# Two 64-row matmuls in place of two 128-row matmuls for the expert shift of the first phase

## What is computed

```python
logits = (jnp.einsum('tzd,ed->tze', x, phi_w) + phi_b).reshape(t, z, n, p)   # n = 64 experts, p = 32 slots
D = jax.nn.softmax(logits, axis=3)       # over the slots of an expert
C = jax.nn.softmax(logits, axis=2)       # over the experts of a slot
X_tilde = jnp.einsum('tznp,tzd->npd', D, x)
```

## Time and profile before

| | |
|---|---|
| median of 3 runs | 1187.13 us |
| span of the profiled execution, first to last instruction | 1184.2 us |
| runs above that span | 2.9 us |
| TensorE busy | 1144.7 us, 97% |
| VectorE busy | 1050.1 us, 89% |
| ScalarE busy | 981.7 us, 83% |
| GpSimd busy | 958.9 us, 81% |

### The profile page before, as it was taken

How to read it: one execution, slowest core, us unless ns; L and a number is a source line. 1 busy time by engine, 2 the same in 40 slices (tenths; PEclk the granted TensorE clock), 3 DMA queues, 4 the chain that set the end, 5 groups by cost and what they waited for, 6 DMA issues and landing times. The chain is left out here.

```text
span 1184.2 us, 17639 instructions
## 1 busy us (share of the span) xinstructions
PE 1144.7 (97%) x5097; PEld 787.9 (67%) x5097; DVE 1050.1 (89%) x1608; ACT 981.7 (83%) x2128; POOL 958.9 (81%) x770
## 2 busy tenths in 40 slices
PE   5999999999999999999989999999999999999996
PEld 3666666565666666666457777777777777777764
DVE  7999999999999999999767888888888888888887
ACT  5877877877766766766668999999999999999998
POOL 3998999898999999999788777878777788877751
PEclk9999999999999999999999999999999999999999
DMA  4445435434424432443754444344444444444420
GB/s 131 152 152 200 141 140 182 153 128 164 155 109 160 155 133 113 161 156 129 225 188 154 131 142 143 119 147 128 142 143 143 131 128 134 141 128 142 142 72 18
DMA packets 125263, 167.36 MB, mean 141 GB/s; under 512 B 7536, under 2 KB 102000, under 8 KB 125040
## 3 DMA queue, kind: packets, MB, share of 16 engines
q1 hardware_dynamic: 123984, 165.71, 41.4%
q10 hardware_dynamic: 1184, 0.53, 0.2%
HBM read 90.71 MB, written 75.50 MB: 140 GB/s over the span
## 5 line engine op out<-in xcount | busy, mean ns | idle before, releaser
L146 POOL TENSOR_TENSOR exp_slots_loaded<-exp_slots_loaded,slot_max 128x1024 f32<-128x1024 f32 x128 | 323.2, 2545 | 6.6 <-DMA exp_slots_loaded<-exp_slots 3.2
L858 POOL TENSOR_TENSOR dd<-ed,rz 128x512 f32<-128x512 f32 x256 | 267.6, 1051 | 24.7 <-ACT rz L688 23.4
L563 PE MATMUL acc<-dd,xns 128*128 128x512 f32 x512 | 261.1, 592 | 0.7 <-POOL dd L858 0.7
L1917 DVE TENSOR_TENSOR clo<-ct,chi 128x512 fp32r<-128x512 f32 x256 | 171.5, 681 | 24.3 <-ACT chi L1585 21.6
L176 POOL TENSOR_TENSOR ch<-exp_slots_loaded 128x512 f32<-128x512 f32 x128 | 165.9, 1296 | 32.0 <-ACT exp_slots_loaded L666 30.9
L795 DVE TENSOR_REDUCE mr<-lg 128x16 fp32r<-128x512 f32 x256 | 168.0, 685 | 19.3 <-PE lg L506 16.9
L657 ACT ACTIVATE ed<-lg 128x512 f32<-128x512 f32 x256 | 145.6, 594 | 40.3 <-PE lg L540 38.4
L666 ACT ACTIVATE exp_slots_loaded<-lg 128x512 f32<-128x512 f32 x256 | 145.5, 594 | 26.4 <-PE lg L549 24.4
L1585 ACT ACTIVATE chi<-ct 128x512 fp32r<-128x512 f32 x256 | 147.7, 597 | 11.8 <-PE ct L1219 8.3
L1219 PE MATMUL ct<-identity,exp_slots_loaded 128*128 128x128 f32 x1024 | 150.9, 273 | 5.6 <-POOL exp_slots_loaded L146 3.1
L811 DVE TENSOR_REDUCE zd<-ed 128x32 f32<-128x1024 f32 x128 | 154.6, 1208 | 1.5 <-ACT ed L657 1.5
(11 more groups left out here) (315 smaller groups left out, 2500.2 us busy)
## 6 DMA issues: line engine op xcount, KB each, us to landing
exp_slots<-exp_slots_loaded SPq DMA_DIRECT2D x128, 512.0 KB, 3.4
exp_slots_loaded<-exp_slots SPq DMA_DIRECT2D x128, 512.0 KB, 3.5
xns<-xn_rows SPq DMA_DIRECT2D x128, 64.0 KB, 1.9
b_xraw<-in_xT SPq DMA_DIRECT2D x16, 256.0 KB, 3.8
out_t<-b_ti SPq DMA_DIRECT2D x15, 256.0 KB, 2.1
expert_w_late<-in_expert_w SPq DMA_DIRECT2D x5, 512.0 KB, 11.1
xn_rows<-slot_sum SPq DMA_DIRECT2D x8, 256.0 KB, 2.5
expert_w_early<-in_expert_w SPq DMA_DIRECT2D x3, 512.0 KB, 5.8
```

Source lines behind the costliest of these rows:

```text
L146: e.tensor_tensor(rows, rows, joined(SM, b)[:, h].unsqueeze(2).broadcast_to([P, TPB, GC * EPC, NP]), ALU.mult).then_inc(s_we)
L563: e.matmul(acc[k][:, :], xns[v % RX][:, :], dd[v % RX][:, bank(k)], start=tile == 0, stop=tile == NT - 1, skip_group_check=True).then_inc( ...
L858: e.tensor_tensor(dd[v % RX][:, bank(k)].rearrange("q (n p) -> q n p", p=NP), ed[v % RD][:, bank(k)].rearrange("q (n p) -> q n p", p=NP), ...
L1917: e.tensor_tensor(clo[g % RC][:, :], ct[c % 2][:, :], hi_f32(chi[g % RC][:, :]), ALU.subtract).then_inc(c_l)
```

## The change

`mr` gets a new layout: bank 0's 16 expert maxima stay in columns 0 to 15, bank 1's 16 go to columns 64 to 79, the slot maxima stay in 32 to 63; everything else is zero (so all of `mr` is zeroed once, and the wait for that moves from TensorE to VectorE). The pattern `S1M` shrinks to 512 columns: rows 0 to 63 serve bank 0, rows 64 to 127 serve bank 1. Each `shift_experts` matmul now contracts only the 64 rows of its bank. `S2M` keeps its shape with its rows rearranged. GpSimd writes five patterns in place of three (four of them over 512 columns). In TensorE's order `shift_experts(2, 0)` and `(2, 1)` now stand together, ahead of `logits(3, 1)`.

```diff
-        S1M = sb(front, "shift_experts", [P, HS], F32R)
+        S1M = sb(front, "shift_experts", [P, BANK], F32R)
...
-        PATTERNS = 7
+        PATTERNS = 9
...
-            shifts = dd[1:3]
+            shifts = [dd[1][:, 0:BANK], dd[2]]
+
+            def rows_of(k):
+                return slice(k * G, (k + 1) * G)
+
+            def experts_of(k):
+                return slice(k * G, k * G + HN // 2)
...
-                e.activation(S1M[:, :], shifts[0][:, :], ACT.Copy).then_inc(s_sc)
+                e.activation(S1M[:, :], shifts[0], ACT.Copy).then_inc(s_sc)
...
-                    e.memset(hi_f32(mr[b][:, G:P]), 0.0).then_inc(s_zero)
+                    e.memset(hi_f32(mr[b][:, :]), 0.0).then_inc(s_zero)
...
-                pattern(1, shifts[0][0:32, :].rearrange("r (n p) -> r n p", p=NP), -1.0, [[-1, HN], [0, NP]])
-                pattern(2, shifts[1][0:32, :].rearrange("r (n p) -> r n p", p=NP), 1.0, [[-1, HN], [0, NP]])
-                pattern(3, shifts[1][HN:HN + 32, :].rearrange("r (n p) -> r n p", p=NP), -1.0, [[0, HN], [-1, NP]])
+                for k in range(2):
+                    pattern(1 + k, shifts[0][k * G:k * G + 32, :].rearrange("r (n p) -> r n p", p=NP), -1.0,
+                            [[-1, HN // 2], [0, NP]])
+                for k in range(2):
+                    pattern(3 + k, shifts[1][k * G:k * G + 32, bank(k)].rearrange("r (n p) -> r n p", p=NP), 1.0,
+                            [[-1, HN // 2], [0, NP]])
+                pattern(5, shifts[1][HN:HN + 32, :].rearrange("r (n p) -> r n p", p=NP), -1.0, [[0, HN], [-1, NP]])
...
                         e.wait_ge(s_mx, MX * (v + 1))
-                        if v < 2:
-                            e.wait_ge(s_zero, v + 1)
                         e.transpose(tr[v % 2], hi_f32(mr[v % 2][:, :]), IDENT[:, :]).then_inc(s_tr)
...
-                        e.matmul(lg[v % 2][:, bank(k)], mt[v % 2][:, :], S1M[:, bank(k)], start=False, stop=True,
+                        e.matmul(lg[v % 2][:, bank(k)], mt[v % 2][rows_of(k), :], S1M[rows_of(k), :], start=False, stop=True,
...
                 for i in range(-3, UNITS // TPB + 3):
+                    shift_experts(i - 2, 2, 0)
+                    shift_experts(i - 2, 2, 1)
                     logits(i - 2, 3, 1)
-                    shift_experts(i - 2, 2, 1)
                     x_tilde(i - 2, 0, 0)
...
                     logits(i - 1, 3, 0)
-                    shift_experts(i - 1, 2, 0)
...
                         e.wait_ge(s_l, 2 * v + k + 1)
-                        e.tensor_reduce(mr[v % 2][:, k * HN // 2:(k + 1) * HN // 2], lg[v % 2][:, bank(k)].rearrange("q (n p) -> q n p", p=NP),
+                        if v < 2 and k == 0:
+                            e.wait_ge(s_zero, v + 1)
+                        e.tensor_reduce(mr[v % 2][:, experts_of(k)], lg[v % 2][:, bank(k)].rearrange("q (n p) -> q n p", p=NP),
```

## The result

The change makes the kernel slower: 1199.7 us (1198.23 to 1200.08, 4 runs) against 1187.18 us (1187.02 to 1187.49, 4 runs), ratio 1.0105, 95% interval 1.0093 to 1.0116. That is 12.5 us more; 1202 us was forecast. The span of the profiled execution went from 1184.2 to 1197.9 us. The lines of the first phase's loop have new numbers (the slot sums keep L188): shift_experts is L548, shift_slots L557, x_tilde L571, the transpose L540, logits L514 to L516.

The account below looks back on a forecast made before the run. TensorE's order was taken to bound the first phase; 28.5 groups at 0.54 us added 15.4 us to the 1184.2 us span, and 2.9 us to the median gave 1202 us. Likeliest case 1194 to 1212; 8-in-10 range down to 1172.

Parts of the forecast that it names:

- The bound: First phase: TensorE's order sets the pace, with about 0.4 us of waits in 17 us.
- The stall: Each shift_experts pair: 0.20 us entering and 0.20 leaving the 64-row form, so 0.63 us in place of 0.46; chance 0.55.
- The units: Cost in each unit of a group: 0.20, 0, 0.17 and 0.17 us for units 0 to 3, sum 0.54.
- The count of groups: First phase: 28.5 of the 32 groups pay 0.54 us each, 15.4 us; VectorE hides it from 40 to 100 us.
- The step from span to time: From profiled span to median of runs: 2.9 us added, 1199.6 to 1202.5 us.
- The moved pair: Unit 2: bank 1's shift moves ahead of three logits matmuls, whose readers on VectorE do not wait; 0.
- the wait: VectorE's new wait is for its own zeroing, done 15 us before; 0.
- S2M: The S2M pattern keeps its size; 0.
- The start: GpSimd's patterns before the phase: two more instructions fit into its 0.86 us wait for the bias; 0.
- No stall: Rival for the shift_experts pair: it takes 0.23 us, giving 1177 us, or 1162 if waits give way; chance 0.35.
- half of it: Rival for the shift_experts pair: 0.10 us in and out, loads hidden, pair 0.43 us, 1188.5 us; chance 0.10.
- loads in a row: Rival: the halves' weights load one after the other, pair 0.74 us, 23 us more, 1210 us; within the 0.55.

Follow-up runs that it names:

- full_rows: The changed kernel, but each shift_experts matmul contracts all 128 rows again, with S1M two banks wide; 1187.14 us, ratio 0.9997 to the kernel before.
- swap_after: The changed kernel, with turn_max of unit 2 moved behind x_tilde(3, 1) of the group before; 1196.38 us, ratio 1.0084 to the kernel before.
- same_half: The changed kernel, but both matmuls of each shift_experts pair contract rows 0 to 63; 1222.26 us, ratio 1.0294 to the kernel before.

## Why the prediction was right

- *The bound.* TensorE's pace was the bound of the phase: what was added to its time beyond its waits came out at the end, and what was taken from its waits did too.
- *The stall.* Sized at 0.20 us in and 0.20 out from one exit of the 32-column form; measured 0.20 and 0.21. The pair takes 0.63 to 0.64 us (0.63 forecast). That the same price holds on the way in was an assumption, now shown.
- *The units.* Taking TensorE's real starts from transpose to transpose (means over 300 to 500 us), unit 0's stretch grew from 4.87 to 5.07 us, unit 1's stayed at 2.94, unit 2's went from 5.70 to 5.86, unit 3's from 3.45 to 3.61. That is 0.20, 0, 0.16 and 0.17 against 0.20, 0, 0.17 and 0.17 forecast.
- *The count of groups*, the term that was mis-sized. 28.5 groups at 0.54 us gave 15.4 us; measured 12.5, and 12.0 from the traces' last slot sums (587.9 and 599.9 us). Of the 12.0, the first slot sum is 0.6 us later, the next ten groups cost 0.22 us each, the five around 300 us, where the first half of the columns ends, 1.5 us together, and the fifteen behind them 0.52 each. TensorE's waits for VectorE are longer in the early groups than in the quiet group from which I took the cost. Two steps were wrong, and partly made up for each other. I let VectorE hide the whole cost from 40 to 100 us because it is full there, but a full VectorE hid only part of it. And I let that stretch end at 100, though the statistics go on for some 150 us more. A stretch's price has to be read from that stretch.
- *The step from span to time.* I added the 2.9 us of the table of the kernel before; the profiled execution after took 1199.68 us with a span of 1197.9, 1.8 us more. So 1.1 of the 2.8 us by which the sum's 1202.5 us is too high lie here and not in the phase. The spans are 13.7 us apart and the last slot sums 12.0; the 1.7 us behind them are within what executions of the kernel before differ by (spans of 1183.0 to 1187.5 us).
- *The moved pair, the wait, S2M.* 0, as full_rows shows. *The start:* five patterns take 4.67 us in place of 4.06, that is 0.3 us for each further instruction, under the 0.43 us that I allowed. GpSimd still waits 0.73 us for the bias behind them; they also began 0.54 us sooner than before, without which the wait would be 0.2 us:

```profile
3.13 4.67 POOL L427 TENSOR_SCALAR_AFFINE_SELECT dd<-dd 32x512 f32<-32x512 f32 x5
8.54 1.04 POOL L440 TENSOR_TENSOR dd<-dd,bias 128x512 f32<-128x512 f32 x1 [0.73 <-DVE bias L332]
```

- *The rivals.* No stall (0.35), half of it (0.10) and loads in a row (part of the 0.55) are excluded by the rows of the pair: 0.64 us, both loads in one row at 343.60. By the rule of the Trainium skill that a change of tiling mode drains the TensorE (TensorEngine Tiling (Array Packing), Key Properties), the trace agrees; the page states no price, and here it is about 0.09 us before a weight load may begin and 0.11 us of a load that nothing covers, at each change.

What stays open: whether the 0.09 us is one fixed time or depends on what streams before. It was the same behind fp32r logits and after the shifts, and with 32 rows; all of these stream 512 columns. Behind the 128 columns of the middle stage it was about 0.09 us too, but at one place alone, and no run varied the length. Why swap_after gained more by its medians than in its trace is open too.

## What to carry to other kernels

Splitting the array's rows lets two matmuls run together, but here, at a granted clock of 1.00, each stay in that form costs about 0.4 us: one pair of 512-column matmuls saves only 0.23 us and loses, three pairs in a row win nearly 0.3 us. Gather such matmuls into one stay, or leave them whole. And before pricing a new stall, look at the next wait behind it in the same queue, in each stretch of the phase: in unit 1 a wait of 0.23 us took up all of it, and filling that very wait by exchanging two instructions gained 4 us, where the change under study lost 12.5.

## What was not expected of the hardware

A contraction over 96 rows runs at the pace of 128 (403 ns mean, 1186.57 us), with no stall and weight loads of 0.19 us as before; 32 rows cost what 64 cost (499 ns mean, 1200.04 us against 1199.70). The weight loads of the two halves start together (one row of 0.19 us for both), where the two loads for the same half in same_half take 0.29 us together.
